# Residual terms by matrix products and wedge measures one chunk at a time, in an attention and mixture block on one core

## Chip, cores, metric

The kernel runs on one core of one Trainium2 chip. Metric: device microseconds of one execution. Before the change the median of 3 runs is 665.44 us (664.79 to 666.22). The engines are written as in the profile: PE (matrix products), PEld (its weight loads), DVE (vector), ACT (scalar), POOL (GpSimd), SP (issues the DMAs).

## Reference

Two batches of 2048 tokens with 128 features go through one attention block and one mixture of experts, with a residual each.

```python
h = _layernorm(x) * (1 + ca) + sa
x = x + ga * attn(h)          # attn: hidden_states + output + 0.1 * quantum_output
h = _layernorm(x) * (1 + cb) + sb
x = x + gb * ffn(h)           # 16 routed experts (top 4 of 2 groups of 4) + 2 shared ones

# attn(h): token positions qp = h @ Wtq.T + btq (two columns)
diff = qp[:, :, None, :] - qp[:, None, :, :]
dist_sq = sum(diff * diff)
forward_bias = 0.5 * (1 + cos(arctan2(diff[..., 1], diff[..., 0])))
valid = (dist_sq <= mean + 1.25 * std) & causal
weights = softmax(where(valid * forward_bias == 0, -inf, scores))   # q k^T / sqrt(128)
output = (weights @ v) @ Wo.T + bo
r_embed = qp / max(norm(qp), 1e-12)
quantum_output = r_embed @ Wfq.T + bfq
return hidden_states + output + 0.1 * quantum_output
```

Since `hidden_states` is h, the attention residual holds ga * (h + r_embed terms + constants) beside the context. These are the residual terms (the code calls them base). A pair is masked when it is too far apart, not causal, or lies in a thin wedge in which the forward bias is zero. The wedge test is |dy| / small - dx, scaled by 2^90: the kernel calls this value a measure.

## The kernel before

**Order of the work.** All engines walk the same program (`run`). Batch 0's inputs come first, in 25 pieces k = 0 to 24. Then batch 0's attention goes in slots n. Then come 144 mixture steps s, 72 for each batch (18 experts times 4 chunks of 512 tokens). Beside the steps of batch 0 run the inputs of batch 1 (steps 0 to 24) and its attention (one slot a step from step 25). The last 72 steps run alone. Each engine executes its own list in order and waits on semaphores; nothing is planned at run time.

**Attention.** A row i is 128 queries. Its keys are cut in chunks c of up to 512 columns, causally: 40 chunks m per batch, 28 of 512 columns and four each of 128, 256 and 384. In slot n, PE makes the distance test (L914, and L916 for the diagonal block) and the scores (L805 to L807) of chunk n, turns the probabilities of an earlier chunk (L939) and multiplies a turned one by v (L954). DVE takes the minimum of distance test and measure into `pen` (L1328), adds it to the scores with a running maximum (L1333), and finishes a row (L1303, L1304, L1308, then statistics for the second norm). ACT copies the turned chunk (L699) and takes the exponential (L705).

**Measures.** ACT writes |dy| into the row buffer (`rise`, L636). In batch 0's rows 0 to 13, which are 32 of its 40 chunks, DVE combines it with dx in one instruction with two SBUF inputs (L1322). In the other 8 chunks and in all of batch 1, ACT also writes dx (L642) and POOL subtracts (L538, `measure`). The buffer holds three whole rows; `RISE_AT` says in which slot a row's chunks may be written again, so that some slots have two measures and some have none.

**Residual terms.** POOL makes them in `base`, in four groups of 4 rows per batch, each of 8 instructions over 128x512 (L516, L512 three times, L503, L525 twice with L503 in between). Group 0 is in input pieces 18 to 22, groups 1 to 3 are spread over attention slots (`BASE_AT`). The constants for it are spread over the partitions by DVE in `spread_terms` (L1163 to L1173), after PE has made them (L797, L857).

**Other work of POOL.** It splits the expert weights in high and low parts (`split`, L489 to L491, four lots), takes roots (L475, L480, L481) and, in the mixture, weighs the hidden values (`weigh`, L580).

## Time and profile before

| | us |
|---|---|
| median of 3 runs | 665.44 |
| profiled execution | 664.28 |
| its span | 662.5 |
| PE busy | 568.8 (86%) |
| DVE busy | 512.1 (77%) |
| ACT busy | 362.5 (55%) |
| POOL busy | 362.1 (55%) |
| mean granted clock of PE, of full speed | 0.951 |

The span goes from the first to the last instruction; 1.8 us of the profiled execution lie around it. By the timelines there are four stages: inputs of batch 0 up to 69.7 us; its attention, whose last rows and routing end at about 195 us; the first 72 mixture steps with batch 1 beside them up to about 500 us; the last 72 steps. A busy share says how much an engine does, not whether others wait for it; that is read from the idle time and its releaser. Durations of neighbouring instructions overlap by up to 0.1 us on ACT and DVE and more on PE, where the distance from start to start is the better price.

### The profile page before, as it was taken

The numbers are of one execution on the slowest core, as the hardware profiler recorded it, in microseconds if no ns is written. First come the engines' busy times: TensorE is split into PE (matmuls) and PEld (weight loads), VectorE is DVE, ScalarE is ACT, GpSimd is POOL, SyncE is SP. The second block draws the span as 40 slices with busy tenths as digits, with TensorE's granted clock in tenths as the row PEclk, the third lists the DMA queues.
The fourth block names the chain that finished last, engine by engine and source line by source line (L and its number), as shares of the span: only waits on it lengthen the run. The fifth ranks groups of instructions, "written<-read, shape, count | busy, mean of one in ns | idle before, by whom it ended". The sixth has DMA issues, their size and how long they took to land.

```text
span 662.5 us, 10953 instructions
## 1 busy us (share of the span) xinstructions
PE 568.8 (86%) x3524; PEld 342.4 (52%) x3524; DVE 512.1 (77%) x1448; ACT 362.5 (55%) x722; POOL 362.1 (55%) x325
## 2 busy tenths in 40 slices
PE   2846878887877899898989999799988599999995
PEld 1734445565653454354545555465554365656563
DVE  3588899997776688656776675756976999898887
ACT  0623567687642633356775868655455355555552
POOL 4459455844104452869977677733314355555553
PEclk9997679898987799899998999999999999999999
DMA  6501000000004121131112220122100000000000
GB/s 187 159 2 35 1 0 1 1 0 1 1 13 115 69 72 45 63 96 49 63 48 60 69 65 32 51 63 63 49 1 16 2 1 17 2 17 2 17 1 17
DMA packets 21840, 26.01 MB, mean 39 GB/s; under 512 B 2628, under 2 KB 11864, under 8 KB 21784
## 3 DMA queue, kind: packets, MB, share of 16 engines
q1 hardware_dynamic: 21784, 25.33, 13.1%
q8 instruction: 28, 0.46, 0.3%
q14 instruction: 28, 0.23, 0.1%
HBM read 23.09 MB, written 2.23 MB: 38 GB/s over the span
## 4 chain that ended last, share of the span: by engine, by line
PE 42%; DVE 34%; issue 8%; ACT 7%; POOL 6%; SPq 1%; DMA 1%; DVEq 0%; ACTq 0%; POOLq 0%
PE bank L805 7%; PE bank L1053 7%; PE bank L806 7%; PE bank L807 6%; DVE row L1322 4%; PE bank L954 4%; DVE stage L1536 4%; ACT stage L745 4%; DVE pen L1328 3%; DVE row L1333 3%; DVE ysb L1515 2%; PE bank L939 2%; POOL sw L580 2%; PE bank L844 2%; PE bank L914 2%
## 5 line engine op out<-in xcount | busy, mean ns | idle before, releaser
L594 POOL TENSOR_TENSOR gp<-stage,gp 128x512 f16<-128x512 f32 x72 | 83.6, 1161 | 73.6 <-ACT gp L762 73.6
L580 POOL TENSOR_TENSOR sw<-hid,gp 128x512 f32<-128x512 f32 x64 | 81.4, 1271 | 76.9 <-DVE hid L1462 70.4
L1462 DVE SCALAR_TENSOR_TENSOR hid<-stage,bank 128x512 f32<-128x512 f32 x72 | 49.2, 684 | 63.5 <-ACT stage L745 62.1
L745 ACT ACTIVATE stage<-bank 128x512 f32<-128x512 f32 x144 | 84.7, 588 | 22.9 <-PE bank L807 22.6
L762 ACT CAST gp<-stage 128x512 f16<-128x512 f32 x72 | 44.4, 617 | 72.8 <-DVE stage L1536 72.8
L538 POOL TENSOR_TENSOR row<-row,dx 128x512 f32<-128x512 f32 (+3 forms) x48 | 54.6, 1141 | 54.3 <-ACT dx L642 54.0
L699 ACT COPY ptr<-bank 128x512 f32<-128x512 f32 (+2 forms) x80 | 41.5, 518 | 78.2 <-PE bank L939 77.6
L1053 PE MATMUL bank<-stage,wd 128*128 128x512 f32 x144 | 76.7, 615 | 7.2 <-DVE ysb L1467 7.2
L954 PE MATMUL bank<-v,ptr 128*128 128x128 f32 x544 | 77.0, 283 | 3.3 <-DVE x L1308 3.3
L954 PEld LDWEIGHTS bank<-v,ptr 128*128 128x128 f32 x544 | 70.9, 200 | 5.3 <-issue 3.9
L1515 DVE SCALAR_TENSOR_TENSOR ysb<-bank,comb,ysb 128x128 f32<-128x128 f32 x240 | 67.1, 342 | 0.1
L805 PE MATMUL bank<-row,gp 128*128 128x128 f16 x288 | 52.3, 220 | 12.4 <-DVE ysb L1515 9.0
L1536 DVE SCALAR_TENSOR_TENSOR stage<-bank,stage 128x512 f32<-128x512 f32 x72 | 49.7, 690 | 16.1 <-ACT stage L745 13.4
L805 PE MATMUL bank<-h,wu 128*128 128x512 f16 x144 | 55.5, 385 | 5.8 <-DVE stage L1492 5.7
L705 ACT ACTIVATE row<-row,nmx 128x512 f32<-128x512 f32 (+2 forms) x80 | 52.7, 659 | 9.8 <-DVE nmx L1338 9.8
L1492 DVE TENSOR_TENSOR stage<-bank,sw 128x512 f32<-128x512 f32 x64 | 44.0, 687 | 16.1 <-POOL sw L580 10.6
L805 PE MATMUL bank<-h,wg 128*128 128x512 f16 x144 | 55.6, 386 | 0.2
L806 PE MATMUL bank<-h,wg 128*128 128x512 f16 x144 | 55.6, 386 | 0.0
L807 PE MATMUL bank<-h,wg 128*128 128x512 f16 x144 | 55.5, 385 | 0.0
L806 PE MATMUL bank<-h,wu 128*128 128x512 f16 x144 | 55.3, 384 | 0.0
L807 PE MATMUL bank<-h,wu 128*128 128x512 f16 x144 | 55.3, 384 | 0.0
L1328 DVE SCALAR_TENSOR_TENSOR pen<-bank,row 128x512 bf16<-128x512 f32 (+2 forms) x80 | 48.5, 606 | 7.3 <-PE bank L914 4.2
(256 smaller groups left out, 1315.9 us busy)
## 6 DMA issues: line engine op xcount, KB each, us to landing
gp<-shares SPq DMA_DIRECT2D x64, 256.0 KB, 3.1
out_x<-x SPq DMA_DIRECT2D x8, 256.0 KB, 2.3
stage<-in_L_ffn_gate_w SPq DMA_DIRECT2D x1, 576.0 KB, 7.5
stage<-in_L_ffn_up_w SPq DMA_DIRECT2D x1, 576.0 KB, 4.2
stage<-in_L_ffn_gate_w SPq DMA_DIRECT2D x1, 448.0 KB, 6.9
stage<-in_L_ffn_up_w SPq DMA_DIRECT2D x1, 448.0 KB, 3.6
row<-in_L_wmod SPq DMA_DIRECT2D x1, 384.0 KB
stage<-in_L_ffn_sh_gate_w SPq DMA_DIRECT2D x1, 128.0 KB, 5.6
```

What stands on the lines that cost most here:

```text
L538: pool.tensor_tensor(o, o, dx[:, pooled(b, m) % 2, 0:w], ALU.subtract).then_inc(measure_ready, 1)
L580: pool.tensor_tensor(sw[:, s % 2, :], hid[:, s % 2, :], wb[:, n % HELD_WEIGHTS, :], ALU.mult)\
L594: pool.tensor_tensor(gp[:, n % HELD, 1, :], act_g[:, s % 2, :], gp[:, n % HELD, 0, :], ALU.subtract)\
L745: act.activation(sg[:, s % 2, :], gate_bank(s)[:, :], func, scale=half_of / (H_UP * W_UP))\
L805: mm(out_bank, weights[0], data[0], start=start, stop=False)
L806: mm(out_bank, weights[0], data[1], start=False, stop=False)
L807: return mm(out_bank, weights[1], data[0], start=False, stop=stop)
L954: last = mm(ring(b, 3, i)[:, 0:P], ptr[:, m % 2, k * P:(k + 1) * P], v[:, j, :], start=(j == 0), stop=(j == i))
L1053: mm(bank[6][:, :], wd[:, d % EX, :], act_g[:, d % 2, :], start=(d % EX == 0), stop=(d % EX == EX - 1)).then_inc(down_made, 1)
L1328: dve.scalar_tensor_tensor(out=pen[:, n % 2, 0:w], in0=ring(b, 1, n)[:, 0:w], scalar=0.0, in1=o[:, c * W:c * W + w], op0=ALU.min, op1=ALU. ...
L1515: last = dve.scalar_tensor_tensor(out=own, in0=y, scalar=weight, in1=own, op0=ALU.mult, op1=ALU.add)
L1536: dve.scalar_tensor_tensor(out=act_g[:, s % 2, :], in0=up_bank(s)[:, :], scalar=G_UP / (H_UP * W_UP), in1=sg[:, s % 2, :], op0=ALU.mult, o ...
```

## The change

- `base` leaves POOL. For each block of 128 tokens PE multiplies h (transposed, in `hT`) by a diagonal matrix of the gates (L873, f32) and adds 21 rows of features times constants (L874, bf16) in the same PSUM block: 16 blocks per batch, in pieces 21 to 24. DVE adds four blocks at once to x (L1290).
- For that the left features get 21 more columns (a copy of the unit vectors and ones), `quant`, `rest` and `parts` are 7 wide instead of 5, and the set-up on DVE makes the diagonals and the constants in three bf16 parts. `spread_terms` becomes one copy (`turned_terms`). In PE's set-up eight passes of L797 and one turn fall away.
- The row buffer is a ring of twelve pieces of 512 columns. Measure m is written six slots ahead of its use, one per slot; the first six in piece 24.
- All 80 measures are made by ACT (|dy|, dx) and POOL. L1322 of DVE is gone.

On POOL, from batch 0's second root (`sdv`) on: first before, then after. `share`, `terms` and `unit` belong to `base`; `row<-row,dx` is a measure; `wg` and `wu` are the split weights.

```order
L475 TENSOR_TENSOR sdv<-var,half 128x1
L489 TENSOR_TENSOR wg<-stage,w_up 128x1152
L490 TENSOR_TENSOR stage<-stage,w_up 128x1152
L491 TENSOR_TENSOR wg<-stage,wg 128x1152
L516 TENSOR_TENSOR share<-x,mv 128x512
L512 TENSOR_TENSOR share<-share,rs 128x512
L512 TENSOR_TENSOR share<-share,terms 128x512 x2
L503 TENSOR_TENSOR x<-x,share 128x512
L525 TENSOR_TENSOR share<-terms,unit 128x512
```

```order
L480 TENSOR_TENSOR sdv<-var,half 128x1
L494 TENSOR_TENSOR wg<-stage,w_up 128x1152
L495 TENSOR_TENSOR stage<-stage,w_up 128x1152
L496 TENSOR_TENSOR wg<-stage,wg 128x1152
L504 TENSOR_TENSOR row<-row,dx 128x128
L504 TENSOR_TENSOR row<-row,dx 128x256
L504 TENSOR_TENSOR row<-row,dx 128x384
L504 TENSOR_TENSOR row<-row,dx 128x512 x2
L504 TENSOR_TENSOR row<-row,dx 128x128
```

The split of the weights stays where it was; behind it stand measures, which wait for ACT, in the place of `base`.

On ACT at the start of batch 0's attention, before and after. `row<-yb,nyi` is |dy|, `dx<-xb,nxi` is dx, `row,rsum<-row,nmx` the exponential.

```order
L636 ACTIVATE row<-yb,nyi 128x128 [waits spread_ready1,spread_ready0]
L636 ACTIVATE row<-yb,nyi 128x256
L636 ACTIVATE row<-yb,nyi 128x384
L705 ACTIVATE row,rsum<-row,nmx 128x128 [waits max_ready]
L699 COPY ptr<-bank 128x128 [waits probs_turned]
```

```order
L598 ACTIVATE row<-yb,nyi 128x512
L603 ACTIVATE dx<-xb,nxi 128x512 [waits rise_ready,measure_ready]
L598 ACTIVATE row<-yb,nyi 128x128
L603 ACTIVATE dx<-xb,nxi 128x128 [waits rise_ready,measure_ready]
L598 ACTIVATE row<-yb,nyi 128x512
L603 ACTIVATE dx<-xb,nxi 128x512 [waits rise_ready,measure_ready]
L666 ACTIVATE row,rsum<-row,nmx 128x128 [waits max_ready]
L598 ACTIVATE row<-yb,nyi 128x256
L603 ACTIVATE dx<-xb,nxi 128x256 [waits rise_ready,measure_ready]
L660 COPY ptr<-bank 128x128 [waits probs_turned]
```

Seven pairs now stand ahead of the first exponential (the last three are shown), where three single instructions stood.

On PE in the mixture steps beside which batch 1's values are made, after the change. `wg` and `wu` are the experts' products, `vh,hT` the values, `diag,hT` and `trows,flT` the residual terms.

```order
L766 MATMUL bank<-h,wu 128x512
L767 MATMUL bank<-h,wu 128x512
L768 MATMUL bank<-h,wu 128x512
L829 MATMUL bank<-vh,hT 128x128 x4
L873 MATMUL bank<-diag,hT 128x128
L874 MATMUL bank<-trows,flT 128x128
L873 MATMUL bank<-diag,hT 128x128
L874 MATMUL bank<-trows,flT 128x128
L873 MATMUL bank<-diag,hT 128x128
L874 MATMUL bank<-trows,flT 128x128
```

The rows L873 and L874 (four of each per step, in four steps) are new; the others stood there before.

```diff
@@ -50,7 +52,8 @@
-ROWS = 3
+UNITS = 12
+AHEAD = 6
...
@@ -77,12 +80,6 @@
-RISE_AT = {CHUNKS_BEFORE[i - ROWS + 1] + CHUNKS_ROW[i - ROWS]: i for i in range(ROWS, BLK)}
...
...
@@ -159,8 +153,9 @@
         x3 = sb("x3", [P, 3])
-        terms = sb("terms", [P, NB, 4, P])
-        share = sb("share", [P, PER, P])
+        gcol = sb("gcol", [P, NB]); gside = sb("gside", [P, 2, NB]); diag = sb("diag", [P, NB, P])
+        tcol = sb("tcol", [P, NB, 3]); trest = sb("trest", [P, NB, 3]); tpart = sb("tpart", [P, 3, NB, 3], BF16)
+        tall = sb("tall", [P, NB, FEAT_LEFT], BF16); trows = sb("trows", [FEAT_LEFT, NB, P], BF16)
         stage = sb("stage", [P, 2, PIECE, P])
...
@@ -307,19 +301,24 @@
                     if 0 <= n < SLOTS:
                         attention(b + 1, n)
+        def unit_of(m):
+            k, o = divmod(m % UNITS, CH)
+            return row[:, k, o * W:(o + 1) * W]
...
-            return b * NCH + m - POOL_FROM + 1
+            return b * NCH + m + 1
+        def base_bank(b, g):
+            return bank[(5, 6, 7, 5)[g] if b == 0 else 7]
...
@@ -490,51 +495,12 @@
-            def base(b, g, part_of):
-                if g == 0 and part_of == 0:
-                    pool.wait_ge(set_dve, 4)
-                    pool.wait_ge(unit_ready, b + 1)
-                    pool.wait_ge(norm_ready, 2 * BLK * b + BLK)
-                own = x[:, b * BLK + g * PER:b * BLK + (g + 1) * PER, :]
...
-                lot = slice(g * PER, (g + 1) * PER)
-                if part_of == 0:
-                    chain.step(pool.tensor_tensor(share[:, :, :], own, spread_token(mv[:, lot, 0:1]), ALU.subtract))
-                    chain.settle()
-                    change(spread_token(rs[:, lot].unsqueeze(2)), ALU.mult)
-                if part_of == 1:
-                    change(spread(3), ALU.mult)
-                    change(spread(2), ALU.add)
-                if part_of in (2, 3):
-                    n = part_of - 2
-                    chain.step(add_to_x()); chain.settle()
-                    chain.step(pool.tensor_tensor(share[:, :, :], spread(n),
-                                                  spread_token(unit[:, lot, n:n + 1]), ALU.mult))
-                    chain.settle()
-                if part_of == 4:
-                    add_to_x().then_inc(base_ready, 1)
-                    pool.wait_ge(base_ready, CH * b + g + 1)
             def measure(b, m):
                 i, c = CHUNKS[m]
                 w = min(W, (i + 1) * P - c * W)
                 pool.wait_ge(dx_ready, pooled(b, m))
-                o = row[:, i % ROWS, c * W:c * W + w]
+                o = unit_of(m)[:, 0:w]
                 pool.tensor_tensor(o, o, dx[:, pooled(b, m) % 2, 0:w], ALU.subtract).then_inc(measure_ready, 1)
...
@@ -548,21 +514,17 @@
                     power(runit[:, :], nrm[:, :], minus_half[:, :], ROOTS * b + 2)
                 if k == POSITIONS + 4:
                     power(sdv[:, :], var[:, :], half[:, :], ROOTS * b + 3)
-                if BASE <= k < BASE + 5:
-                    base(b, 0, k - BASE)
-                if k == PIECES - 1 and b:
-                    for m in range(2):
+                if k == PIECES - 1:
+                    for m in range(AHEAD):
                         measure(b, m)
             def attention(b, n):
-                for m in MEASURES_AT.get(n, ()):
-                    if by_pool(b, m):
-                        measure(b, m)
+                if n + AHEAD < NCH:
+                    measure(b, n + AHEAD)
                 if n in ROOT_AT:
                     lot = slice(ROOT_AT[n] * PER, (ROOT_AT[n] + 1) * PER)
+                    pool.wait_ge(norm_ready, 2 * BLK * b + BLK)
                     norm_root(lot, ROOTS * b + 4 + ROOT_AT[n])
-                if n in BASE_AT:
-                    base(b, *BASE_AT[n])
                 if b == 0 and n in WEIGHTS_AT:
                     split(WEIGHTS_AT[n])
...
@@ -630,17 +592,16 @@
                 i, c = CHUNKS[m]
                 w = min(W, (i + 1) * P - c * W)
                 lot = slice(c * W, c * W + w)
-                if i >= ROWS:
-                    act.wait_ge(probs_turned, NCH * b + CHUNKS_BEFORE[i - ROWS] + min(c + 1, CHUNKS_ROW[i - ROWS]))
-                act.activation(row[:, i % ROWS, lot], yb[:, lot], ACT.Abs, bias=nyi[:, i:i + 1]).then_inc(rise_ready, 1)
-                if by_pool(b, m):
-                    if pooled(b, m) > 2:
-                        act.wait_ge(measure_ready, pooled(b, m) - 2)
-                    act.wait_ge(rise_ready, NCH * b + m + 1)
-                    act.activation(dx[:, pooled(b, m) % 2, 0:w], xb[:, lot], ACT.Identity, bias=nxi[:, i:i + 1])\
-                       .then_inc(dx_ready, 1)
+                if m >= UNITS:
+                    act.wait_ge(probs_turned, NCH * b + m - UNITS + 1)
+                act.activation(unit_of(m)[:, 0:w], yb[:, lot], ACT.Abs, bias=nyi[:, i:i + 1]).then_inc(rise_ready, 1)
+                if pooled(b, m) > 2:
+                    act.wait_ge(measure_ready, pooled(b, m) - 2)
+                act.wait_ge(rise_ready, NCH * b + m + 1)
+                act.activation(dx[:, pooled(b, m) % 2, 0:w], xb[:, lot], ACT.Identity, bias=nxi[:, i:i + 1])\
+                   .then_inc(dx_ready, 1)
...
@@ -684,7 +645,7 @@
-                    for m in range(2):
+                    for m in range(AHEAD):
                         rise(b, m)
...
@@ -700,12 +661,12 @@
...
-                for m in MEASURES_AT.get(n, ()):
-                    rise(b, m)
+                if n + AHEAD < NCH:
+                    rise(b, n + AHEAD)
...
@@ -896,6 +857,23 @@
                         if g:
                             pe.wait_ge(spread_ready[0], CH * b + g)
                         mm(bank[2][:, :], selx[:, :], lot, start=True, stop=True).then_inc(spread_made[0], 1)
+                if BASE <= k < BASE + CH:
+                    g = k - BASE
+                    if b == 0:
+                        pe.wait_ge(set_dve, 4)
+                        if g == CH - 1:
+                            pe.wait_ge(base_added, 1)
+                    else:
+                        pe.wait_ge(comb_copied, CH)
+                        if g:
+                            pe.wait_ge(base_added, CH * b + g)
+                    for j, i in enumerate(range(g * PER, (g + 1) * PER)):
+                        dst = base_bank(b, g)[:, j * P:(j + 1) * P]
+                        mm(dst, hT[:, i * P:(i + 1) * P], diag[:, b, :], start=True, stop=False)
+                        last = mm(dst, flT[FEAT_UNIT:FEAT_LEFT, i * P:(i + 1) * P], trows[FEAT_UNIT:FEAT_LEFT, b, :],
+                                  start=False, stop=True)
+                    last.then_inc(base_made, 1)
             def attention(b, n):
                 lag = behind(b)
...
@@ -1139,6 +1118,18 @@
                 step(dve.scalar_tensor_tensor(out=gbc[:, :, :, :].rearrange("p b g d -> p (b g d)"),
                                                op0=ALU.add, op1=ALU.mult))
+                gate = md[:, 2, :]
+                step(dve.tensor_scalar(gside[:, 0, :], gate, 0.0, 2.0, ALU.is_ge, ALU.mult))
+                step(dve.scalar_tensor_tensor(out=gside[:, 1, :], in0=gate, scalar=-1.0, in1=gate,
+                                              op0=ALU.mult, op1=ALU.max))
+                settle()
+                step(dve.tensor_scalar(gside[:, 1, :], gside[:, 1, :], NEAR, None, ALU.max))
+                settle()
+                step(dve.scalar_tensor_tensor(out=gcol[:, :], in0=gside[:, 0, :], scalar=-1.0, in1=gside[:, 1, :],
+                                              op0=ALU.add, op1=ALU.mult))
+                settle()
+                for b in range(NB):
+                    step(dve.tensor_scalar(diag[:, b, :], ident[:, :], gcol[:, b:b + 1], None, ALU.mult))
...
@@ -1152,25 +1143,28 @@
-                for n in range(3):
-                    step(dve.tensor_scalar(x3b[:, n, :], ones[:, :], x3[:, n:n + 1], None, ALU.mult))
+                for b in range(NB):
+                    step(dve.tensor_scalar(tcol[:, b, :], x3[:, :], gcol[:, b:b + 1], None, ALU.mult))
+                settle()
+                step(dve.tensor_copy(tpart[:, 0, :, :], tcol[:, :, :])); settle()
+                step(dve.tensor_tensor(trest[:, :, :], tcol[:, :, :], tpart[:, 0, :, :], ALU.subtract)); settle()
...
+                    step(dve.tensor_copy(tall[:, b, FEAT_LEFT - 3:FEAT_LEFT], tpart[:, :, b, 2]))
                 settle()
                 dve.sem_inc(set_dve, 1)
...
@@ -1229,11 +1223,8 @@
                     step(dve.tensor_scalar(nyi[:, :], quant[:, :, 2], -HUGE, None, ALU.mult))
                     dve.wait_ge(root_ready, ROOTS * b + 2)
-                    if b:
-                        dve.wait_ge(base_ready, CH * b)
-                    dve.tensor_tensor(unit[:, :, :], qp[:, :, :], runit[:, :].unsqueeze(2).broadcast_to([P, BLK, 2]),
-                                      ALU.mult).then_inc(unit_ready, 1)
+                    step(dve.tensor_tensor(quant[:, :, 5:7], qp[:, :, :],
+                                           runit[:, :].unsqueeze(2).broadcast_to([P, BLK, 2]), ALU.mult))
                 if k == POSITIONS + 5:
                     dve.wait_ge(root_ready, ROOTS * b + 3)
...
@@ -1287,6 +1282,13 @@
                         dve.wait_ge(spread_made[0], CH * b + g + 1)
                         dve.tensor_copy(xb[:, g * W:(g + 1) * W], bank[2][:, :])\
                            .then_inc(spread_ready[0], 1)
+                if BASE <= k < BASE + CH:
+                    g = k - BASE
+                    dve.wait_ge(base_made, CH * b + g + 1)
+                    own = x[:, b * BLK + g * PER:b * BLK + (g + 1) * PER, :]
+                    dve.tensor_tensor(own, own, base_bank(b, g)[:, :].rearrange("p (k d) -> p k d", d=P), ALU.add)\
+                       .then_inc(base_added, 1)
             def split_input(b, g):
...
@@ -1312,25 +1314,18 @@
                 if n < NCH:
                     i, c = CHUNKS[n]
                     L = (i + 1) * P
-                    o = row[:, i % ROWS, :]
-                    if by_pool(b, n):
-                        dve.wait_ge(measure_ready, pooled(b, n))
-                    else:
-                        lot = slice(c * W, min((c + 1) * W, L))
-                        dve.wait_ge(rise_ready, NCH * b + n + 1)
-                        step(dve.scalar_tensor_tensor(out=o[:, lot], in0=xb[:, lot], scalar=nxi[:, i:i + 1],
-                                                      in1=o[:, lot], op0=ALU.add, op1=ALU.subtract, reverse1=True))
-                        settle()
                     w = min(W, L - c * W)
+                    o = unit_of(n)
+                    dve.wait_ge(measure_ready, pooled(b, n))
                     dve.wait_ge(dist_made, NCH * b + n + 1)
                     dve.scalar_tensor_tensor(out=pen[:, n % 2, 0:w], in0=ring(b, 1, n)[:, 0:w], scalar=0.0,
-                                             in1=o[:, c * W:c * W + w], op0=ALU.min, op1=ALU.min)\
+                                             in1=o[:, 0:w], op0=ALU.min, op1=ALU.min)\
                        .then_inc(dist_used, 1)
                     dve.wait_ge(dist_used, NCH * b + n + 1)
                     dve.wait_ge(scores_made, NCH * b + n + 1)
-                    dve.tensor_tensor_reduce(o[:, c * W:c * W + w], ring(b, 0, n)[:, 0:w], pen[:, n % 2, 0:w],
+                    dve.tensor_tensor_reduce(o[:, 0:w], ring(b, 0, n)[:, 0:w], pen[:, n % 2, 0:w],
...
```

## Rows read from the trace of the kernel before

**Rows 1.** Busy time by stage: length, then us (count) of each engine, granted clock, DMA

```profile
0.00:69.70 69.70, 39.86 (x184) 29.64 (x184) 45.41 (x122) 24.01 (x43) 44.13 (x60) 0.91 0.33 91
69.70:165.30 95.60, 79.76 (x479) 50.91 (x479) 87.36 (x222) 67.98 (x152) 51.35 (x38) 0.88 0.00 1
...
262.00:293.90 31.90, 29.56 (x152) 15.42 (x150) 17.92 (x27) 14.03 (x25) 22.08 (x19) 0.95 0.25 75
293.90:334.10 40.20, 37.95 (x187) 19.45 (x186) 29.37 (x83) 27.45 (x60) 37.06 (x34) 1.00 0.18 53
334.10:358.00 23.90, 21.14 (x104) 11.33 (x102) 16.02 (x41) 14.96 (x31) 17.42 (x15) 0.93 0.14 46
358.00:424.00 66.00, 66.00 (x347) 37.33 (x346) 45.31 (x112) 49.11 (x100) 48.25 (x42) 1.00 0.21 60
```

**Rows 2.** Whom ACT waited for in 69.7 to 165.3: us in total, times, longest

```profile
ACT ptr L699 <- PE bank L939: 12.8, 16, 1.7
ACT row L705 <- DVE nmx L1338: 7.6, 7, 2.1
ACT xn L624 <- POOL nmr L481: 5.3, 3, 3.1
...
ACT hT L612 <- PE bank L816: 0.7, 1, 0.7
```

**Rows 3.** Timeline of DVE and then POOL, batch 0's inputs: start, us, instruction

```profile
42.63 1.45 DVE L1170 TENSOR_TENSOR terms<-row,gbc 128x256 f32<-128x256 f32 x1
44.41 1.92 DVE L1170 TENSOR_TENSOR terms<-row,gbc 128x256 f32<-128x256 f32 x1
46.36 2.53 DVE L1173 TENSOR_TENSOR terms<-terms,gbc 128x128 f32<-128x128 f32 x2
...
51.50 1.19 DVE L1246 TENSOR_TENSOR rest<-quant,parts 128x80 f32<-128x80 f32 x1
...
59.03 1.29 DVE L1263 TENSOR_SCALAR fl<-parts 128x48 bf16<-128x48 bf16 x1
...
41.70 2.10 POOL L489 TENSOR_TENSOR wg<-stage,w_up 128x1152 f16<-128x1152 f32 x1
...
46.13 2.42 POOL L491 TENSOR_TENSOR wg<-stage,wg 128x1152 f16<-128x1152 f32 x1
...
51.27 2.66 POOL L512 TENSOR_TENSOR share<-share,terms 128x512 f32<-128x512 f32 x2
```

**Rows 4.** The same kind of DVE row in batch 1's inputs

```profile
257.12 0.24 DVE L1246 TENSOR_TENSOR rest<-quant,parts 128x80 f32<-128x80 f32 x1
```

**Rows 5.** Groups, 69.7 to 165.3, L642 of 290 to 470: busy us, mean ns; idle before

```profile
L1322 DVE SCALAR_TENSOR_TENSOR row<-xb,nxi,row 128x512 f32<-128x512 f32 (+3 forms) x32 | 30.5, 952 | 0.5 <-ACT row L636 0.5
...
L636 ACT ACTIVATE row<-yb,nyi 128x512 f32<-128x512 f32 x26 | 18.4, 709 | 0.0
...
L642 ACT ACTIVATE dx<-xb,nxi 128x512 f32<-128x512 f32 (+3 forms) x40 | 26.3, 658 | 5.2 <-POOL row L538 1.7
```

**Rows 6.** Timeline of ACT where POOL already makes batch 0's measures

```profile
146.81 0.71 ACT L636 ACTIVATE row<-yb,nyi 128x512 f32<-128x512 f32 x1
147.55 0.72 ACT L642 ACTIVATE dx<-xb,nxi 128x512 f32<-128x512 f32 x1
...
149.36 0.71 ACT L636 ACTIVATE row<-yb,nyi 128x512 f32<-128x512 f32 x1
```

**Rows 7.** Timeline of PE: batch 0's inputs, then batch 1's inputs beside mixture steps

```profile
58.85 1.92 PE L869 MATMUL bank<-vh,hT 128*128 128x128 f32 x8
...
265.42 1.07 PE L884 MATMUL bank<-identb,fl 128*27 128x128 bf16 x16
266.42 0.39 PE L805 MATMUL bank<-h,wg 128*128 128x512 f16 x1
...
286.12 1.05 PE L869 MATMUL bank<-vh,hT 128*128 128x128 f32 x8
287.01 0.38 PE L805 MATMUL bank<-h,wg 128*128 128x512 f16 x1
```

**Rows 8.** Chain of waits from 293.9 to 312, by line

```profile
by line: POOL sw L580 28.1%; POOL share L512 19.6%; POOL row L538 18.9%; POOL x L503 13.5%; issue 8.5%; POOL share L525 6.2%; POOL share L516 5.5%; POOLq L576 0.4%
```

**Rows 9.** Whom DVE (293.9 to 334.1), then PE (334.1 to 358) waited for

```profile
DVE stage L1492 <- POOL sw L580: 5.9, 6, 1.7
...
PE bank L1053 <- DVE ysb L1467: 2.8, 1, 2.8
```

94 lines of the change are left out of this document (44 added, 50 removed).

## The prediction

> **What bounds the kernel now.** I read four views: busy time by stage, then the waits of single engines inside a stage, then timelines at the places that the change touches, then the chain of waits where it names POOL.
>
> The stages have different limits [rows 1]. In the inputs of batch 0 (0 to 69.7 us) no engine is full on the average; the limit has to be read from the timeline. In batch 0's attention up to 165.3 us, DVE is busy 87.4 of 95.6 us, PE 79.8 and ACT 68.0: DVE sets the pace. In the steps with batch 1 beside them the limit is PE from 358 to 424 us (66.0 of 66), and nearly so from 293.9 to 334.1 (37.95 of 40.2), where POOL is busy 37.1. There the chain of waits runs over POOL: L580 28.1%, L538 18.9%, and the residual lines L512, L503, L525 and L516 together 44.8% up to 312 us [rows 8]. The last 72 steps hold nothing that the change touches.
>
> **Part 1: inputs of batch 0.** POOL's residual terms and its weight split read SBUF while DVE runs instructions with SBUF inputs, and each slows down to about one POOL instruction. L1170 takes 1.45 and 1.92 us beside splits of 2.1 to 2.4 us, L1246 takes 1.19 us beside a `share` instruction [rows 3]; the same L1246 in batch 1's inputs, with POOL idle, takes 0.24 us [rows 4]. The change removes `spread_terms` (41.6 to 48.9 us, of it 1.45 + 1.92 + 2.53 us in three rows) for one short copy, and removes the residual terms that stood beside DVE from 49.0 to 60.5 us. It does not remove the split (41.7 to 48.6 us). New on DVE are some 13 short instructions ahead of it, about 1.2 us (0.08 to 0.24 us each, the smaller value where nothing waits between them), so the split moves to about 42.9 to 49.8 us.
>
> Then `rest` and `parts` come beside the split. At one per POOL instruction, as in rows 3, DVE gets three of the contended ones through by 49.8 us; two others, one product for kT (0.75 us) and nine feature writes of about 0.2 us are free after it: 49.8 + 0.5 + 0.7 + 1.5 = 52.5 us, against 60.5 us before (the row at 59.03, which ends at 60.3, and two short copies behind it). What follows (kT, turns, spreads) is unchanged. Term: -8.0 us, bounds -10 (one more gets in between) and -6 (one less, longer set-up).
> The Trainium skill, "SBUF — State Buffer", section "Who interferes with whom", has the pair of ports as a lock held for a whole instruction, also against a DVE instruction with two SBUF inputs. By that rule the same three instructions wait for the split, and the term stays -8; the trace's 1.19 against 0.24 us agrees.
>
> **Part 2: batch 0's attention.** DVE loses L1322: 30.5 us for 32 chunks [rows 5]. That is no gain by itself, because ACT takes the work over. Up to its slot 33 (165.3 us) ACT was busy 68.0 us [rows 1]. It now makes all 40 pairs by that slot: 34 more dx of 0.658 us (mean over all sizes) and two more |dy| of 0.709 us [rows 5], so 22.4 + 1.4 = 23.8 us, 91.8 in all, and about 0.05 us of handing over between each pair (0.74 us from start to start for 0.71 us of work in rows 6), 1.7 us: 93.5 us. The window was 95.6 us. So ACT becomes the bound, and what counts is how much of its idle time of 27.6 us is left. It waited 12.8 us for PE's turns, 7.6 us for DVE's row maximum, 5.3 us for POOL's roots, 0.7 for the norm's turn [rows 2]. The second goes with the DVE pace. The third goes too: the root is asked for a slot before ACT needs it, and DVE is no longer late. Of PE's 12.8 us most were PE's own waits for DVE. Where POOL already makes measures in this batch, ACT goes from one |dy| to the next in 2.55 us with almost no idle time [rows 6]. I leave 6 us: about 0.8 us at each of three norms, 3.6 us at PE's turns and the start. That makes 99.5 us, +3.9, less some 0.4 us in slots 34 and 35, which lose their two pairs: +3.5 us. Bounds: no idle time at all, -2; all of PE's 12.8 us and the norm's 0.7 us kept, +12.
>
> What lies beside it: the six pairs of piece 24 (about 6.7 us on ACT) and PE's residual products start together after the last spread. PE's group costs 8 passes of an f32 product of 128 columns, 0.89 us from start to start at full clock and up to 1.92 us at the lower one, and four bf16 ones, for which the nearest row is a turn of 16 in 1.00 us, so 0.25 us [rows 7]: 1.15 us, and with some switching between kinds 1.3 us; four groups 5.3 us. They are hidden behind ACT's 6.7 us here, unless the clock is low (8.7 us, 2 us more). POOL's splits of 7 us in slots 8 and 17 could hold ACT's dx (two buffers), but ACT's norm work (about 3 us and its wait) falls in the same slots; cost 0, and 2 us each if that cover is gone.
>
> **Part 3: steps with batch 1 beside them.** PE's 16 + 16 products stand in four steps around 277 to 293 us, where PE goes from one product to the next without idle time. Not hidden: 4 x 1.3 = +5.3 us (bounds 4.6 and 6). In the last of them ACT makes six pairs in a row, 6.7 us instead of 1.8 us for two (or so), and the silu of the next step but one waits behind them; PE has about 3 us of other steps to run: +2 us (0 to +5). From 293.9 us on POOL loses the residual terms. DVE waited 5.9 us for L580 there [rows 9] and PE was idle 2.25 us as shown [rows 1]; I take -4.0 us, between the two (bounds -5.9 and -1). From 334.1 to 358 us PE waited 2.8 us for L1467 [rows 9], behind two pairs on ACT in one slot, and was slow afterwards at a lower clock (0.93 in the stretch, rows 1): one pair per slot brings -2.0 us (0 to -3). The wider feature rows of batch 1 cost DVE 0.5 us, less contention around 270 us gives 0.3 back. Together +1.5 us (-4 to +8).
>
> **Sum.** -8.0 + 3.5 + 1.5 = -3.0 us, from the profiled execution's 664.3: 661.3 us. The profiled execution lies 1.2 us under the median of the runs, so the median to expect is 662.5 us.
>
> **Rivals.**
> (a) ACT and PE run side by side without losses. Rows 6 and the small wait for the norm speak for it, the 12.8 us for turns against. Inputs -9, attention -2, third part 4.6 + 0.5 - 5.6 - 2.8 = -3.3: -14.3, so 651 us.
> (b) Slower: ACT as the bound of batch 0's attention keeps its waits for PE's turns, as each turn now stands between ACT's own exponential and its copy. Place: slots 0 to 33; price 93.5 + 12.8 + 0.7 = 107.0 us, +11.4; it decides as soon as ACT's idle time there passes about 9 us. -8.0 + 11.4 + 1.5 = +4.9: 670 us. For it: rows 2. Against it: rows 6.
> The Trainium skill, "ScalarE: Activation LUTs", section "Rules for kernel authors", gives adds and products to VectorE, not ScalarE. The rule speaks against this change, and (b) is what it would look like.
> (c) The third part pays and gives little back: PE is already full at 94% from 293.9 to 334.1, so POOL's relief brings only 2 us, the six pairs cost 5 and the products 6: 6 + 5 - 2 - 1.5 = +7.5, in all -8.0 + 3.5 + 7.5 = +3.0: 668.5 us.
>
> **How the numbers follow.** Chances: my forecast 0.47, (a) 0.13, (b) 0.25, (c) 0.15. The difference that a measurement of this kernel can tell is 0.2%, 1.3 us: faster is below 664.1, slower above 666.8. My forecast's own range is 657 to 667.5; of its 0.47 I give 0.33 to faster, 0.10 to the same, 0.04 to slower. (a) is all faster. (b) gives 0.02, 0.03 and 0.20, (c) 0.02, 0.03 and 0.10. Faster 0.50, same 0.16, slower 0.34. The range that holds the time 8 times in 10 reaches to both sides' cases: 653 to 671.
>
> **What would show it.** Features ready (the last feature write of DVE in batch 0's inputs) at 52 to 53 us instead of 60.5. Batch 0's attention, from the first |dy| of ACT to the sigmoid, 98 to 101 us instead of 95.6, ACT busy over 90 of them and DVE under 65. PE's new lines about 1.3 us a group with no idle time around them. POOL busy about 25 of 40 us in the first ten slots of batch 1, and no longer in the chain. I am wrong if ACT is idle over 10 us in batch 0's attention, or if that stretch is shorter than before, or if the first 72 steps change by more than 5 us.

## The result, and the profile after

The change makes the kernel slower: 681.23 us (median of 4 runs, 678.57 to 683.87) against 665.83 us (664.79 to 668.24), a ratio of 1.0227 with a 95% interval of 1.0202 to 1.0252. The prediction was 662.5 us. The profiled execution of the changed kernel has a span of 678.6 us, 16.1 us over that of before.

Busy time and instructions of each engine after (the table of before has the shares to compare):

```profile
span 678.6 us, 11120 instructions
PE 593.6 (87%) x3608; PEld 358.7 (53%) x3608; DVE 485.2 (72%) x1436; ACT 381.2 (56%) x754; POOL 307.9 (45%) x287
```

DVE has 27 us less work, POOL 54 us less, ACT 19 us more, PE 25 us more. PE is the engine with the most work, and it got more. Whether that is why the time grew is not in these sums; it is read stage by stage. Both kernels run the same 72 mixture steps beside batch 1, so each step's down product (L1053 before, L1032 after) is a mark that can be laid beside its partner. The marks, in us from the span's start:

| from, to | before | after | difference |
|---|---|---|---|
| start, first \|dy\| of ACT | 69.7 | 62.3 | -7.4 |
| first \|dy\|, end of the sigmoid | 95.6 | 108.6 | +13.0 |
| sigmoid, step 19 | 112.3 | 112.4 | +0.1 |
| step 19, step 23 | 13.15 | 22.05 | +8.9 |
| step 23, step 26 | 8.97 | 13.26 | +4.3 |
| step 26, step 29 | 14.05 | 11.47 | -2.6 |
| step 29, step 36 | 33.56 | 32.63 | -0.9 |
| step 36, step 71 | 151.21 | 151.82 | +0.6 |
| step 71, end | 163.99 | 164.03 | 0.0 |

The same stages in the view of busy time by stretch (PE, PEld, DVE, ACT, POOL, then the granted clock), where [rows 1] has those of before:

```profile
0.00:62.30 62.30, 39.76 (x175) 28.23 (x175) 38.26 (x132) 23.97 (x42) 25.23 (x45) 0.93 0.38 102
62.30:170.90 108.60, 94.49 (x525) 60.77 (x525) 64.30 (x193) 89.05 (x188) 60.21 (x52) 0.82 0.00 1
...
283.30:305.35 22.05, 22.05 (x113) 13.92 (x112) 8.13 (x12) 6.61 (x13) 5.73 (x6) 0.95 0.20 58
305.35:318.61 13.26, 10.49 (x42) 4.54 (x41) 6.34 (x17) 8.96 (x19) 10.15 (x10) 0.87 0.14 44
```

In batch 0's attention (second row) DVE fell from 87.4 to 64.3 us, as the change means it to, and the stretch is 13 us longer: no engine fills it. In the third row PE is busy all the time. In the fourth, only 13 us long, PE is idle 2.8 us and its granted clock is 0.87, where it was 1.00 before.

**What PE does ahead of batch 0's attention.** PE's timeline, in each row the start, the duration and the product (the first of 16 blocks, the last, and the first distance test):

```profile
61.50 0.80 PE L873 MATMUL bank<-diag,hT 128*128 128x128 f32 x2
62.23 0.28 PE L874 MATMUL bank<-trows,flT 21*128 21x128 bf16 x1
62.44 0.80 PE L873 MATMUL bank<-diag,hT 128*128 128x128 f32 x2
...
76.33 0.28 PE L874 MATMUL bank<-trows,flT 21*128 21x128 bf16 x1
77.48 0.26 PE L893 MATMUL bank<-frT,flT 27*128 27x128 bf16 x1 [0.87 <-DVE x L1290]
```

Sixteen blocks at 0.94 us from start to start, 3.76 us a group, 15.1 us in all. The granted clock was 0.50 from 62 to 78 us (1.2 of 2.4 GHz); PE had been busy 14.5 of the 20 us from 40 to 60, and was busy without a gap from 61.5 us on. What ACT did meanwhile, from its timeline:

```profile
62.33 0.40 ACT L598 ACTIVATE row<-yb,nyi 128x128 f32<-128x128 f32 x1 [1.08 <-DVE xb L1283]
...
69.97 0.72 ACT L603 ACTIVATE dx<-xb,nxi 128x512 f32<-128x512 f32 x1
78.97 0.40 ACT L666 ACTIVATE row<-row,nmx 128x128 f32<-128x128 f32 x1 [8.27 <-DVE nmx L1333]
```

Its seven pairs took 8.4 us and were done at 70.7 us. Then it waited 8.3 us for the first row maximum, which waits for a distance test, which stands behind the products on PE and, for another 0.9 us, behind DVE's add of the last group (L1290, in the last row above). The first `pen` came 0.8 us after the first |dy| before the change, and 15.8 us after it now.

**What a group costs in batch 1.** PE's timeline between the marks of steps 19 and 20, where nothing is idle:

```profile
285.83 1.06 PE L829 MATMUL bank<-vh,hT 128*128 128x128 f32 x8
286.72 0.39 PE L873 MATMUL bank<-diag,hT 128*128 128x128 f32 x2
287.04 0.22 PE L874 MATMUL bank<-trows,flT 21*128 21x128 bf16 x1
287.20 0.49 PE L873 MATMUL bank<-diag,hT 128*128 128x128 f32 x2
...
288.77 0.23 PE L874 MATMUL bank<-trows,flT 21*128 21x128 bf16 x1
288.93 0.39 PE L766 MATMUL bank<-h,wg 128*128 128x512 f16 x1
```

From 286.72 to 288.93 is 2.21 us. The eight passes of L829, of the same kind and size, take 0.89 us; eight passes of L873 and four bf16 ones between them take 2.21. The first pair stands behind f32 work and takes 0.32 us from start to start, the others stand behind a bf16 product and take 0.42.

**The burst.** ACT's timeline from the last copy of the values to the next silu (L706), which the next row of DVE waits for:

```profile
302.69 0.58 ACT L633 COPY v<-bank 128x512 f32<-128x512 f32 x1 [1.80 <-PE bank L829]
303.18 0.40 ACT L598 ACTIVATE row<-yb,nyi 128x128 f32<-128x128 f32 x1
...
309.52 0.40 ACT L603 ACTIVATE dx<-xb,nxi 128x128 f32<-128x128 f32 x1
309.83 0.58 ACT L706 ACTIVATE stage<-bank 128x512 f32<-128x512 f32 x1
```

DVE's timeline at the same place, the row that takes that silu:

```profile
310.44 0.69 DVE L1457 SCALAR_TENSOR_TENSOR hid<-stage,bank 128x512 f32<-128x512 f32 x1 [4.95 <-ACT stage L706]
```

PE's timeline behind it, the next product that waits for DVE:

```profile
311.79 0.39 PE L766 MATMUL bank<-h,wu 128*128 128x512 f16 x1 [2.77 <-DVE stage L1487]
```

Six pairs, 6.65 us; DVE waits 4.95 us, and PE then 2.8 us for DVE. The other 1.5 us of the 4.3 come after the stall: the granted clock was 0.57 from 313.5 to 316.5 us.

### The profile page after: what moved, and what is told of

The parts are those of the page before. It is cut to its first block, busy times and chain, and to the rows that moved or that the text cites. A ratio compares the mean times of both kernels' runs of the same rounds, so it can differ in the third digit from the quotient of the medians.

```text
span 678.6 us, 11120 instructions
## 1 busy us (share of the span) xinstructions
PE 593.6 (87%) x3608; PEld 358.7 (53%) x3608; DVE 485.2 (72%) x1436; ACT 381.2 (56%) x754; POOL 307.9 (45%) x287
## 4 chain that ended last, share of the span: by engine, by line
PE 58%; DVE 19%; ACT 12%; issue 7%; POOL 2%; SPq 1%; DMA 1%; ACTq 0%; DVEq 0%; POOLq 0%
PE bank L766 10%; PE bank L767 9%; PE bank L768 9%; PE bank L1032 8%; PE bank L933 5%; PE bank L918 3%; ACT row L598 2%; PE bank L873 2%; PE bank L893 2%; DVE ysb L1510 2%; ACT row L666 2%; ACT stage L706 2%; PE bank L805 2%; DVE stage L1531 2%; ACT ptr L660 2%
## 5 line engine op out<-in xcount | busy, mean ns | idle before, releaser
L504 POOL TENSOR_TENSOR row<-row,dx 128x512 f32<-128x512 f32 (+2 forms) x80 | 89.4, 1119 | 121.1 <-ACT dx L603 120.8
L706 ACT ACTIVATE stage<-bank 128x512 f32<-128x512 f32 x144 | 84.8, 589 | 33.8 <-PE bank L768 33.7
L1457 DVE SCALAR_TENSOR_TENSOR hid<-stage,bank 128x512 f32<-128x512 f32 x72 | 49.3, 685 | 66.3 <-ACT stage L706 64.8
L1032 PE MATMUL bank<-stage,wd 128*128 128x512 f32 x144 | 77.1, 618 | 6.6 <-DVE ysb L1462 6.6
L933 PE MATMUL bank<-v,ptr 128*128 128x128 f32 x544 | 79.0, 288 | 3.2 <-DVE x L1310 3.2
L933 PEld LDWEIGHTS bank<-v,ptr 128*128 128x128 f32 x544 | 73.0, 205 | 4.7 <-issue 3.4
L1323 DVE SCALAR_TENSOR_TENSOR pen<-bank,row 128x512 bf16<-128x512 f32 (+2 forms) x80 | 48.4, 605 | 25.6 <-PE bank L893 21.5
L766 PE MATMUL bank<-h,wu 128*128 128x512 f16 x144 | 55.6, 386 | 7.9 <-DVE stage L1487 7.9
L1531 DVE SCALAR_TENSOR_TENSOR stage<-bank,stage 128x512 f32<-128x512 f32 x72 | 49.7, 690 | 16.1 <-ACT stage L706 13.4
L666 ACT ACTIVATE row<-row,nmx 128x512 f32<-128x512 f32 (+2 forms) x80 | 52.7, 658 | 10.2 <-DVE nmx L1333 10.2
L603 ACT ACTIVATE dx<-xb,nxi 128x512 f32<-128x512 f32 (+2 forms) x80 | 52.6, 658 | 7.6 <-ACT row L598 0.4
L918 PE MATMUL bank<-ident,row 128*128 128x128 f32 x272 | 47.7, 294 | 9.7 <-ACT row L666 7.3
L767 PE MATMUL bank<-h,wu 128*128 128x512 f16 x144 | 55.4, 385 | 0.0
```

Source lines behind the costliest of these rows:

```text
L504: pool.tensor_tensor(o, o, dx[:, pooled(b, m) % 2, 0:w], ALU.subtract).then_inc(measure_ready, 1)
L666: act.activation(probs, probs, ACT.Exp, bias=nmx[:, i:i + 1], accum_out=rsum[:, i, c:c + 1]).then_inc(probs_ready, 1)
L706: act.activation(sg[:, s % 2, :], gate_bank(s)[:, :], func, scale=half_of / (H_UP * W_UP))\
L766: mm(out_bank, weights[0], data[0], start=start, stop=False)
L767: mm(out_bank, weights[0], data[1], start=False, stop=False)
L918: last = pe.transpose(ring(b, 2, m)[:, k * P:(k + 1) * P], unit_of(m)[:, k * P:(k + 1) * P], ident[:, :])
```

## The experiments

All are compared with the kernel before, run on the same chip (its medians there are 665.3 to 666.3 us). "Features" is the end of DVE's last feature write. "Pen" is the distance from ACT's first |dy| to DVE's first `pen`. The steps' columns are differences to before.

| kernel | median us | ratio (95%) | features | pen | \|dy\| to sigmoid | 19-23 | 23-26 | 26-29 | 29-36 |
|---|---|---|---|---|---|---|---|---|---|
| before | 665.8 | 1 | 60.5 | 0.8 | 95.6 | 0 | 0 | 0 | 0 |
| after | 681.2 | 1.0227 (1.0202-1.0252) | 52.8 | 15.8 | 108.6 | +8.9 | +4.3 | -2.6 | -0.9 |
| e1 | 674.4 | 1.0130 (1.0108-1.0153) | 52.9 | 9.0 | 98.8 | +5.1 | +5.0 | -2.6 | -0.9 |
| e2 | 669.8 | 1.0101 (1.0042-1.0160) | 52.8 | 3.1 | 98.8 | +1.7 | +7.3 | -2.6 | -0.9 |
| e3 | 682.8 | 1.0275 (1.0247-1.0303) | 61.2 | 1.5 | 105.0 | -0.2 | +6.7 | -1.1 | -0.5 |
| e4 | 676.7 | 1.0162 (1.0141-1.0183) | 53.1 | 15.8 | 105.2 | +9.0 | -0.3 | -2.6 | -1.6 |
| e5 | 657.9 | 0.9862 (0.9831-0.9893) | 49.1 | 0.8 | 98.9 | +0.2 | 0.0 | 0.0 | 0.0 |
| e6 | 667.4 | 1.0004 (0.9986-1.0022) | 49.4 | 0.8 | 94.3 | +1.3 | 0.0 | 0.0 | 0.0 |
| e7 | 665.3 | 0.9994 (0.9964-1.0023) | 53.1 | 10.2 | 97.9 | +5.0 | -0.3 | -2.6 | -1.6 |
| e8 | 668.3 | 1.0035 (1.0013-1.0056) | 52.6 | 10.9 | 101.8 | +5.3 | -0.3 | -2.6 | -1.6 |
| e9 | 678.3 | 1.0189 (1.0123-1.0256) | 53.5 | 15.8 | 105.9 | +8.9 | -0.3 | -2.6 | -0.1 |
| e10 | 663.3 | 0.9956 (0.9934-0.9978) | 50.1 | 1.4 | 98.9 | +0.1 | 0.0 | +0.7 | -1.6 |
| e11 | 672.9 | 1.0120 (1.0059-1.0180) | 48.4 | 10.4 | 108.9 | +4.3 | -0.3 | -2.6 | -1.6 |
| e12 | 659.0 | 0.9898 (0.9870-0.9927) | 49.2 | 0.8 | 98.8 | +0.2 | 0.0 | +0.7 | -1.6 |
| e13 | 659.5 | 0.9901 (0.9868-0.9934) | 49.3 | 0.8 | 99.2 | 0.0 | +1.0 | +0.4 | -0.2 |
| e14 | 668.7 | 1.0018 (0.9986-1.0050) | 53.4 | 10.4 | 102.1 | +5.2 | -0.3 | -2.6 | -0.9 |
| e15 | 657.1 | 0.9869 (0.9847-0.9892) | 48.9 | 1.3 | 98.4 | 0.0 | 0.0 | 0.0 | 0.0 |
| e16 | 662.0 | 0.9949 (0.9930-0.9967) | 53.7 | 0.8 | 96.3 | +0.2 | 0.0 | 0.0 | 0.0 |

The steps' columns repeat to 0.3 us between kernels that do the same there, except where the granted clock differs: 19-23 is +1.3 in e6 (clock 0.84 instead of 0.93 before) and +4.3 in e11 (1.00; 0.96 in e1 and e7). The attention's and the medians move by 2 to 3 us, and the place at which the granted clock falls moves with them.

**e1: the four f32 products of a group first, then the four bf16 ones.**

```diff
 for j, i in enumerate(range(g * PER, (g + 1) * PER)):
     dst = base_bank(b, g)[:, j * P:(j + 1) * P]
-    mm(dst, hT[...], diag[:, b, :], start=True, stop=False)
-    last = mm(dst, flT[...], trows[...], start=False, stop=True)
+    mm(dst, hT[...], diag[:, b, :], start=j == 0, stop=False)
+for j, i in enumerate(range(g * PER, (g + 1) * PER)):
+    dst = base_bank(b, g)[:, j * P:(j + 1) * P]
+    last = mm(dst, flT[...], trows[...], start=False, stop=j == PER - 1)
```

> Changed kernel, but in each group of residual products the four f32 products come first and then the four bf16 ones, with one start for the whole bank. Theory A (changing between f32 and bf16 is what makes a group dear: 0.42 us for an f32 pair behind a bf16 product, 0.16 us for a bf16 one, 2.3 us a group at full clock and 3.76 us at half clock, where the four value products of f32 alone take 0.89 us): a group falls to 1.2 to 1.6 us at full clock, 3 to 4 us are won in batch 1 and 5 to 6 us in batch 0, in all about 672 us. Theory B (the products have this price in any order): a group stays at 2.3 us and the time at 681 us.

674.4 us. PE at step 22 in e1, the same products in the new order:

```profile
290.07 1.06 PE L873 MATMUL bank<-diag,hT 128*128 128x128 f32 x8
291.06 0.39 PE L876 MATMUL bank<-trows,flT 21*128 21x128 bf16 x4
291.39 0.39 PE L766 MATMUL bank<-h,wg 128*128 128x512 f16 x1
```

1.32 us instead of 2.21, at the same full clock. Theory A holds: the alternation costs 0.9 us a group. Steps 19 to 23 lose 5.1 us instead of 8.9, and batch 0's attention is back at 98.8 us; that the median is 2 us above the expected 672 goes with inputs that were 3.9 us slower than those of the changed kernel in this execution. At half clock the order counts for more: a group takes 2.54 us (65.40 to 67.94) instead of 3.76. In batch 0 only the first two groups of e1 ran at half clock; the clock rose in the third, and the four took 8.5 us instead of 15.1. ACT's wait for the first row maximum shrinks from 8.3 us to

```profile
ACT row L666 <- DVE nmx L1335: 1.5, 1, 1.5
```

**e2: the products left out.** One bf16 product over 512 columns stands for each group, so this kernel leaves the residual terms out.

```diff
-for j, i in enumerate(...): mm(... diag ...); last = mm(... trows ...)
+last = mm(base_bank(b, g)[:, :], trows[...], flT[..., i * P:(i + PER) * P], start=True, stop=True)
```

> Changed kernel, the residual terms left out of the computation: a group is one bf16 product over 512 columns, all waits and DVE's four adds stay. If the groups of products stand on the path at their full length (15.1 us in batch 0 to the first pen, 8.9 us in four steps of batch 1), 681 - 14 - 8.5 = 658 us. Rival: in batch 0 ACT's six pairs (6.7 us) and its own pace take over as soon as the products are gone, so that only the 8.3 us are won that ACT waited for the first row maximum: 681 - 8.3 - 8.5 = 664 us. If PE's products did not matter: 681 us.

669.8 us; the rival said 664. In its trace the attention takes 98.8 us from the first |dy| to the sigmoid, of which ACT is busy 88.8:

```profile
63.90:162.80 98.90, 81.30 (x481) 51.56 (x480) 63.62 (x195) 88.78 (x188) 60.35 (x52) 0.85 0.00 1
```

This is the attention that the prediction described (98 to 101 us, ACT as the bound). So the rival's reading is right for batch 0: with the products gone ACT takes over. 4.5 us over the kernel before remain in the median (3 to 11 us by the interval) with only the four stand-ins per batch left. In its trace the sum is -5.7 us (inputs), +3.2 (attention), +0.4 (sigmoid to step 19), +1.7 and +7.3 (steps 19 to 26, the burst above all), -3.5 (26 to 36), +1.5 later.

**e3: ring and measures alone.** The kernel before with parts 2 and 3 of the change.

```diff
-ROWS = 3
+UNITS = 12
+AHEAD = 6
...
-for m in MEASURES_AT.get(n, ()):
-    rise(b, m)
+if n + AHEAD < NCH:
+    rise(b, n + AHEAD)
```

> Kernel before with the ring of twelve pieces and all measures by ACT and POOL (lead of six slots); the residual terms stay on POOL. From the comparison of the two traces: attention of batch 0 -1.9 us (92.9 against 94.7 us from the first pen to the sigmoid), burst of six pairs in batch 1 +4.3 us, step 36 -0.8 us, no residual products: 665.8 + 1.6 = 667.4 us. Rival: POOL, with 51 us of work in the 95.6 us of that attention and 34 more measures of 1.1 us, becomes the bound and DVE waits for it: 670 us or more.

682.8 us, at least as slow as the whole change; the rival's time was right. Batch 0's attention in e3:

```profile
72.30:177.30 105.00, 81.25 (x479) 52.46 (x479) 61.57 (x190) 88.63 (x188) 90.75 (x79) 0.83 0.00 1
```

Whom ACT waited for in it:

```profile
ACT dx L635 <- POOL row L533: 6.7, 6, 1.7
ACT xn L618 <- POOL nmr L476: 4.0, 2, 3.6
ACT ptr L692 <- PE bank L932: 2.2, 5, 0.8
```

POOL and ACT have about 90 us of work each in one loop, and ACT waits for POOL; DVE, which the rival named, waits for POOL's measures only 2.2 us itself. So part 3, with POOL's 32 more measures, needs part 1, which empties POOL (60.2 us busy in the changed kernel's stretch), and part 1 puts its work on PE. The ring alone does not need it (e13 below).

**e4: a lead of two slots** (`AHEAD = 2` in the changed kernel).

> Changed kernel with a lead of two slots instead of six. Theory (the 4.3 us between mixture steps 24 and 26 come from six pairs in a row on ACT, ahead of its silu): two pairs stand there again, -3 to -4 us, about 677.5 us. Rival 1: the loss there is POOL's or the products', no change, 681 us. Rival 2: a pair and POOL's part take 2.7 us, and with two slots of lead DVE waits for measures: over 681 us.

676.7 us. The loss at step 25 is gone (-0.3 instead of +4.3): it was the six pairs. ACT's timeline at the same place; the silu stands behind two pairs:

```profile
306.20 0.51 ACT L603 ACTIVATE dx<-xb,nxi 128x256 f32<-128x256 f32 x1
307.19 0.60 ACT L706 ACTIVATE stage<-bank 128x512 f32<-128x512 f32 x1 [0.48 <-PE bank L768]
```

All kernels with this lead lose 1.2 us at step 62, where the last measures of batch 1 now fall.

**e5: another way to the inputs' gain.** The kernel before, with POOL's work moved away from DVE's and no products.

```diff
-WEIGHTS_AT = {8: 2, 17: 3}
+WEIGHTS_AT = {4: 1, 12: 2, 20: 3}
...
-if b == 0 and k in (NORM, POSITIONS + 5):
-    split(0 if k == NORM else 1)
+if b == 0 and k == NORM:
+    split(0)
...
     pool.wait_ge(unit_ready, b + 1)
+    pool.wait_ge(feat_ready, b + 1)
```

> Kernel before, with the second split of expert weights on POOL moved from the inputs of batch 0 to slot 4 of its attention (the others to slots 12 and 20), and the residual terms of its first four rows held until the features are written. No matrix product for the residual terms, no ring. Theory A (DVE's instructions in the inputs were long because POOL read SBUF beside them): the features are ready at 50 to 53 us instead of 60.5, the attention pays 1 to 3 us for one more split beside DVE's L1322, in all 665.8 - 7.7 + 2 = 660 us. Theory B (the new set-up and products of the change made the inputs shorter, or the clock did): features at about 60 us, time 665 us or more. Theory C (POOL's queue is now late in the attention: the first finished rows wait for residual terms): features at 52, but what is won is lost at the first slots, 665 us.

657.9 us, faster than both kernels. DVE in the inputs of e5, the instructions of [rows 3]:

```profile
43.06 0.41 DVE L1171 TENSOR_TENSOR terms<-row,gbc 128x256 f32<-128x256 f32 x1
...
46.45 0.24 DVE L1247 TENSOR_TENSOR rest<-quant,parts 128x80 f32<-128x80 f32 x1
...
48.93 0.20 DVE L1266 COPY fr<-parts 128x48 bf16<-128x48 bf16 x1
```

0.41 us instead of 1.45 and 1.92, 0.24 instead of 1.19: Theory A. The features are ready 11.4 us earlier, and the attention pays 3.3 us for one more split; the measures (L1322 before) take 33.0 us instead of 30.5, so most of it is there.

**e6: the splits behind the attention** (`WEIGHTS_AT = {34: 1, 36: 2, 43: 3}`, else as e5).

> As e5, but the three later splits stand in slots 34, 36 and 43, behind the part in which DVE is full. Features again at 50 to 53 us. If the splits cost DVE contended instructions (one L1322 takes 2.86 us beside a split instead of 0.74), the attention is shorter than in the kernel before by 2 to 4 us, in all about 656 us. Rival: POOL's roots for the last norms stand behind 7 us of split each, and routing waits for them: +5 us on that, 663 us or more.

667.4 us; the rival's time was right, its reason not. The attention up to the sigmoid takes 94.3 us, 4.6 less than in e5 and 1.3 less than before (measures 26.8 us instead of 30.5). But from the sigmoid to step 0 it loses 13.1 us. That is again DVE beside a split: the first nine instructions of the routing (L1387 to L1401 before) took 2.3 us in all before and 16.1 us in e6, where POOL's three splits stand beside them from 160.5 to 182.0 us. One of them, before and in e6:

```profile
174.32 0.25 DVE L1396 TENSOR_TENSOR ps<-pm 128x48 f32<-128x48 f32 x1
...
170.77 2.13 DVE L1397 TENSOR_TENSOR ps<-pm 128x48 f32<-128x48 f32 x1
```

DVE's next `pen` and maximum stand behind them in its list, and ACT waits for that maximum:

```profile
ACT row L706 <- DVE nmx L1339: 15.7, 1, 15.7
```

**e7: sorted products and a lead of two.** e1 and e4 together.

> Changed kernel with the sorted residual products and a lead of two slots. If the two gains are separate (6.8 us and 4.5 us in the medians of the single runs), 681.2 - 6.8 - 4.5 = 669.9 us, still over the kernel before: ACT stays the bound of batch 0's attention and four groups of products stand ahead of it. If they overlap: 673 us.

665.3 us: the change without its two avoidable losses cannot be told from the kernel before, somewhat better than the sum of the single gains (10 runs, 662.7 to 669.9).

**e8: e7 with DVE's measures back in batch 0's rows 0 to 13.**

> As e7, and the third part of the change undone: in batch 0's rows 0 to 13 DVE makes the measures again. ACT loses 32 dx there (21 us), DVE gains 30 us. Theory A (ACT against DVE as the bound is a wash: 92.9 us against 94.7 us from the first pen to the sigmoid): within 2 us of e7, 668 to 672 us. Theory B (ACT's waits on PE are what costs; with DVE as the bound the products of batch 0 are followed at once by slots at the old pace, and the measures of the first chunks don't wait for ACT): 3 to 5 us faster than e7, 665 to 667 us.

668.3 us, 3.0 us over e7. Theory B fails. The attention takes 101.8 us against 97.9 in e7, but at a clock of 0.83 against 0.87; the intervals of the two ratios overlap. With POOL emptied of the residual terms, the third part is worth between nothing and 5 us.

**e9: the first part alone.** The rows and measures of before with the changed kernel's products.

> The first part of the change alone: residual terms by PE (in the order f32, bf16, f32, bf16 of the change), rows and measures as before. Theory (products cost what the traces show and the other parts matter little while they stand): inputs -7.4, products ahead of batch 0's attention +15.1, an attention at DVE's pace of 94.7 us or 1 to 2 us less because POOL has nothing but splits beside it, products in batch 1 +8.9, no burst: 665.8 - 7.4 + 15.1 - 1.5 + 8.9 = 681 us. Rival: the first part gives back at POOL what it costs, because the waits for POOL's residual terms and measures go: 672 us or less, and then the ring and the measures make the change slow.

678.3 us. The first part alone makes 12.6 of the 15.4 us in the medians; its interval allows 8 to 17. Its 26-29 column has the -2.6 us of POOL's relief, its 23-26 column no burst. From the first `pen` to the sigmoid it takes 90.1 us (94.7 before). ACT has only three |dy| (1.3 us) beside the four groups, and so waits for their whole length, the longest of these waits (the third number):

```profile
ACT row L673 <- DVE nmx L1347: 19.7, 6, 15.3
```

**e10: e5 with the ring at a lead of two**, DVE keeping its measures.

> e5 with the ring of twelve pieces at a lead of two slots; the measures of batch 0's rows 0 to 13 stay with DVE, the residual terms stay with POOL. Theory (the 2.6 us of steps 28 and 29 and the 1.4 us of step 36 come from one measure per slot, not from POOL's residual terms): 657.9 - 4 = 654 us. Rival (they came from POOL, which is busy with residual terms here): 658 us.

663.3 us, slower than e5 and over both the theory's and the rival's time. The -1.6 us between steps 29 and 36 are there, so they belong to one measure per slot; the -2.6 us between 26 and 29 are not (+0.7), so they belong to POOL's relief; e9, with the one and without the other, has -2.6 and -0.1. After step 36 it loses 3.0 us, at step 62 and at a lower clock (0.76 and 0.70, before 1.00) in steps 65 to 67.

**e11: e7 with the split moved as in e5.**

> e7 with the second split of expert weights moved to slot 4 of batch 0's attention. Theory (contention with POOL): features at about 50 us instead of 53, -3 us there, the attention pays up to 1 us, because DVE has no instruction there that the splits hold: 665.3 - 2.5 = 663 us. Rival: with a lead of two slots a split of 7 us holds up POOL's measures, and slots 4 to 8 lose 3 us or more: 666 us.

672.9 us; the rival was right, and by more than it said. Whom DVE waited for in batch 0's attention:

```profile
DVE pen L1325 <- POOL row L504: 22.7, 8, 5.8
DVE pen L1325 <- PE bank L895: 9.5, 6, 3.6
```

In e7 the first of these is 11.5 us. With all measures on POOL, a split of 6.7 us in one of the first slots stops them. The same move of the splits that brings 4.9 us where DVE measures (e15 against e16, same chip) costs 7.6 us in the medians where POOL does (e11 against e7; two chips, the ratios say 4 to 13 us).

**e12: e10 with 8 more chunks by ACT and POOL** (`POOL_FROM = CHUNKS_BEFORE[12]`).

> e10 with batch 0's rows 12 and 13 (8 chunks) also measured by ACT and POOL. If DVE is the bound of that attention up to slot 24: 8 instructions of 0.75 to 0.95 us less, -3 us at most against e10 since ACT gets 5 us more. If ACT and DVE are balanced there already: no change.

659.0 us (658.5 to 664.6 in 5 runs) against 663.3 (660.0 to 664.7 in 10). The traces do not show why: 98.8 us of attention against 98.9, the same steps, and a profiled span (662.9) over e10's (661.3), as the profiled execution is the slowest of e12's five. What the medians differ by stays open.

**e13: e10 with a lead of six and its first six pairs two by two in pieces 22 to 24.**

```diff
-if k == PIECES - 1:
-    for m in range(AHEAD):
+if k >= PIECES - 3:
+    for m in range(2 * (k - PIECES + 3), 2 * (k - PIECES + 4)):
         rise(b, m)
```

> e10 with a lead of six slots, its first six pairs not in one row in piece 24 but two each in pieces 22, 23 and 24. Theory (the burst costs only because the six pairs stand in one row ahead of a silu; a lead of six slots avoids the 1.2 us that a lead of two loses at step 62): no loss at step 25, -0.8 us at step 36, nothing at step 62: 657.9 - 0.8 = 657 us, 6 us faster than e10. Rival: the pairs cost ACT's and PE's time wherever they stand in those steps, 3 us or more over that.

659.5 us. Steps 23 to 26 lose 1.0 us instead of 6.7 (e3, same lead), and step 62 nothing. The burst's price is that of the pairs standing in one row. The -0.8 us of step 36 did not come (-0.2 from 29 to 36).

**e14: the change mended in the same way** (e1 with the pairs in pieces 22 to 24).

> Changed kernel with the sorted products and the six pairs spread over pieces 22 to 24: 674.4 - 5 = 669.5 us if the 5.1 us of step 25 in e1 go and nothing else. It stays slower than the kernel before, because batch 0's products still stand ahead of its attention.

668.7 us (10 runs, 660.3 to 670.9), and 23-26 at -0.3: both as expected. That it is slower than the kernel before is not shown: the ratio is 1.0018 (0.9986 to 1.0050), without the two longest runs, one of which is the profiled one. The four groups in batch 0 took 9.8 us, and ACT waited 3.2 us for the first row maximum.

**e15: e5 again, on the chip of e13.**

> The kernel of e5 once more, on the same chip as e13: 658 us again. If e13 is right with its sum, the two differ by less than 1.5 us.

657.1 us, ratio 0.9869 (0.9847 to 0.9892). Its steps are those of before to 0.1 us. The ring adds no gain to it: e13's median is 2.4 us higher, and the intervals overlap.

**e16: one wait added to the kernel before.** Only `pool.wait_ge(feat_ready, b + 1)` ahead of the first residual terms.

> Kernel before with one wait more: POOL's residual terms of the first four rows start when the features are written; the split of weights stays where it was. What the change does to the inputs, without its products. Theory: spread_terms still stands beside the split (5.9 us in three rows), but from 48.9 us on DVE is alone: features at about 53.5 us, -7 us, attention as before or 1 us longer, 659.5 us. Rival: POOL is then behind with groups 0 and 1, and the first finished rows wait: 663 us or more.

662.0 us, between the theory's and the rival's time. DVE's timeline in its inputs; the `rest` row that took 1.19 us [rows 3] is short:

```profile
50.99 0.24 DVE L1247 TENSOR_TENSOR rest<-quant,parts 128x80 f32<-128x80 f32 x1
...
53.47 0.20 DVE L1266 COPY fr<-parts 128x48 bf16<-128x48 bf16 x1
```

POOL's first residual row waits until the features are written:

```profile
53.97 1.04 POOL L517 TENSOR_TENSOR share<-x,mv 128x512 f32<-128x512 f32 x1 [5.04 <-DVEq L1268]
```

The features are ready 6.9 us earlier, nearly all that the change wins there, with none of its products. The first |dy| comes only 4.0 us earlier in this execution.

## Why the prediction was wrong, step by step

**Part 1, inputs: right.** Predicted -8.0 us with the features at 52 to 53 us; measured -7.4 and 52.8. The features repeat (52.6 to 53.5 us in the eight kernels that share the change's inputs). That the whole stretch came so near is partly luck: the first |dy| is 3.5 to 7.4 us earlier in these eight traces, and the changed kernel's is the largest. The cause was right too: e16 and e5 take POOL's reads away from DVE in another manner, and the same instructions shrink to their price in batch 1 [rows 4]. The Trainium skill, "SBUF — State Buffer", section "Who interferes with whom", has this as a lock on a shared pair of ports that is held for a whole instruction, for a DVE instruction with two SBUF inputs and a GpSimd one that reads SBUF; 0.24 against 1.19 us for one DVE row agrees.

**Part 2, batch 0's attention: the step that failed.** Predicted +3.5 us, measured +13.0. What failed is the price in the sentence "They are hidden behind ACT's 6.7 us here": 5.3 us for the four groups, 8.7 at a low clock. They took 15.1 us, because PE ran at half clock and because f32 and bf16 alternate; sorted, four groups at half clock would be 10.2 us (4 x 2.54).

The cover itself was real, and it ends where ACT's pairs end. ACT's wait for the first row maximum is what sticks out of it. In the kernels with a lead of six, where ACT's seven pairs last 8.0 to 8.4 us, that wait is 8.3 us with 15.1 us of products (after), 3.2 with 9.8 (e14), 1.5 with 8.5 (e1) and nothing with the stand-ins of 2.6 (e2). In e9, with 1.3 us of ACT's work beside 15.1 us of products, it is 15.3 us. So 8.3 of the 9.5 us by which the term was off are located. The rest is not located; the clock may be in it: the stretch is 98.8 us in e1 and e2 at a clock of 0.90 and 0.85, 102.1 in e14 at 0.86 and 108.6 after the change at 0.82.

The estimate of ACT as the bound came out at 99.5 us against 98.8 in e2, but by two errors that cancel: ACT was busy 88.8 us instead of the 93.5 of the sum, and idle 10.0 instead of 6. Two of the three signs of being wrong came: ACT was idle 19.5 us in that stretch, and the first 72 steps changed by over 5 us.

**Part 3, the steps with batch 1: +10.3 us against +1.5; the products' term lies outside its bounds, the three others on the dear side of their forecasts.**
- Products: predicted +5.3 us (1.3 a group), measured +8.9 (2.2 a group). The price was that of the same products in sorted order, which e1 measures at 1.32. [Rows 7] are rows of one kind; the order on PE, shown ahead of the prediction, had the two kinds in turn, and I allowed 0.15 us for it where 0.9 was due.
- The burst: predicted +2 us (0 to +5), measured +4.3, and 5.0 to 7.3 in e1, e2 and e3, where less or nothing of the last group of products (2.2 us after the change) lies beside the pairs. The prediction saw the place and the mechanism (e4 and e13 confirm them). PE is idle 2.8 us, and the lower clock behind the stall, which had no term, makes the rest.
- POOL's relief: predicted -4.0 us, measured -2.6 in every kernel whose residual terms left POOL, and not in e3, e10 and e13 (-1.1, +0.7 and +0.4). From step 26 to 29 DVE waited 4.4 us for POOL's L580; now it waits 2.3 us for ACT's silu. One pair per slot: predicted -2.0 us, measured -0.9 (e10 with the shorter lead: -1.6).

**The rest.** The forecast that POOL leaves the chain and is busy some 25 of 40 us in batch 1's first ten slots is right (23.0 of 40), and so is that the last 72 steps do not change. Rival (b), 670 us, had the right stage and sign but not the cause: ACT waits 5.9 us for PE's turns there, half of before's 12.8. Rival (c), "the third part pays and gives little back", is what happened in batch 1 (+7.5 predicted, +10.3 measured). My chances treated (b) and (c) as alternatives; both stages went wrong at once, and the sum fell outside the range.

The Trainium skill, "ScalarE: Activation LUTs", section "Rules for kernel authors", gives adds and products to VectorE, not ScalarE. With the residual terms off POOL, e7 against e8 does not bear that out here: the kernel with ACT's and POOL's measures is if anything the faster one (0.9994 against 1.0035, the intervals overlap).

## What to carry to other kernels

Work put ahead of a loop is hidden only for as long as the engine that bounds the loop has work of its own beside it: ACT's pairs of 8.4 us hid about as much of the 15.1 us of products, and three |dy| (e9) hid next to nothing. Price a new product in the order in which it will stand: groups of one type first, not in turn, and check what stands ahead of the next activation when a lead is built up. And before moving work to another engine because two engines disturb each other, try moving it in time: one wait (e16) brought nearly all of the features' gain, and the wait and the moved splits (e5, e15) made the kernel 1.3 to 1.4% faster than before, while the whole change made it 2.3% slower.

## What the hardware showed that I had not expected

- f32 and bf16 products in turn cost 2.21 us a group, sorted 1.32 us at full clock; 3.76 and 2.54 us at half clock. The traces show the price, not its cause.
- A run's low-clock phases move: in before, after and e1 to e4 the granted clock from 50 to 55 us was 0.58, 1.00, 0.61, 0.71, 0.50 and 0.66, and the first |dy| came 9.2 to 13.4 us after the features. One stage's gain in one trace is therefore known to 2 or 3 us only.
- Where POOL's splits of 6.7 us stand decides over several us in both directions. Moved from the inputs into the early slots they gained 4.9 us (e15 against e16); with all measures on POOL the same move lost 7.6 us (e11), since the measures stand behind them in POOL's order; and behind the attention (e6) they stretched nine short DVE instructions from 2.3 to 16.1 us, six of them at 2.0 to 2.5 us each.
